# A routed expert layer: f32 matmuls on copied weights against f16 pairs read at the expert's address

## The reference

```python
def _L2_ffn_ref(x, Wr, br, W1, b1, W2, b2):        # (2, 1024) tokens, H=256, F=1024, 8 experts
    probs = softmax(x @ Wr + br); gate = probs * keep      # keep: top-p 0.8
    h = relu(einsum('bth,ehf->betf', x, W1) + b1)          # every expert for every token
    y = einsum('betf,efh->beth', h, W2) + b2
    return einsum('bte,beth->bth', gate, y)

def _L3_ffn_ref(x, gate_w, w1, b1, w2, b2):        # x: layernormed rows
    router_probs = softmax(x_flat @ gate_w)
    expert_idx = argmax(router_probs); expert_w = router_probs[expert_idx]
    for e in range(8):                              # one expert for each token
        h = gelu(x_flat @ w1[e] + b1[e])            # exact gelu
        y = h @ w2[e] + b2[e]
        out = out + where(expert_idx == e, expert_w, 0)[:, None] * y
...
x = x + _L2_ffn_ref(_layernorm(x), ...)
x = x + _L3_xattn_ref(_layernorm(x), ctx_1024, ctx_1024, ..., fside, ...)
x = x + _L3_ffn_ref(_layernorm(x), L3_ffn_gate_w, L3_ffn_w1, L3_ffn_b1, L3_ffn_w2, L3_ffn_b2)
```

## Time and profile before

| | us |
|---|---|
| median of 3 runs | 3391.13 |
| the profiled execution's own time | 3388.76 |
| its span | 3387.2 |
| TensorE busy | 2920.6 (86%) |
| VectorE busy | 2081.2 (61%) |
| ScalarE busy | 1898.3 (56%) |
| POOL busy | 1309.0 (39%) |

### The profile page before, as it was taken

The page is one execution under the profiler, slowest core; times in us unless marked ns, Lnnn a source line. Parts: engine busy times, 40 slices in busy tenths (PEclk is TensorE's granted clock), DMA queues, the critical chain, the costliest instruction groups (busy, mean ns, idle before and its releaser), DMA issues. The chain is left out here.

```text
span 3387.2 us, 67815 instructions
## 1 busy us (share of the span) xinstructions
PE 2920.6 (86%) x26424; PEld 2022.7 (60%) x26425; DVE 2081.2 (61%) x3113; ACT 1898.3 (56%) x2879; POOL 1309.0 (39%) x944
## 2 busy tenths in 40 slices
PE   6769998746979998979998597979999999998596
PEld 3246665424536666446667596766666666667595
DVE  6968887577968883968873223855444444466222
ACT  3448886283658884658884012855555555466131
POOL 2249998020248884148883213810000000055212
PEclk8979998877979999989998798979999999998698
DMA  4611111200022220022222412011000000052512
GB/s 140 230 57 55 54 56 59 91 13 13 1 56 54 57 48 15 1 60 54 54 48 105 153 37 52 2 51 30 26 26 26 26 26 1 1 117 68 213 36 70
DMA packets 218051, 193.17 MB, mean 57 GB/s; under 512 B 126837, under 2 KB 176866, under 8 KB 216738
## 3 DMA queue, kind: packets, MB, share of 16 engines
q1 hardware_dynamic: 210247, 172.30, 17.6%
q0 software_dynamic: 5280, 14.42, 1.3%
q10 hardware_dynamic: 2233, 2.39, 0.2%
HBM read 112.72 MB, written 39.00 MB: 45 GB/s over the span
## 5 line engine op out<-in xcount | busy, mean ns | idle before, releaser
L2667 POOL TENSOR_TENSOR lta_p_lo<-lta_p,lta_p_hi 128x1024 f16<-128x1024 f32 x256 | 538.7, 2131 | 214.7 <-DVE lta_p_hi L2790 214.7
L2862 ACT ACTIVATE lta_p<-lta_banks,lw_gmax 128x512 f32<-128x512 f32 x512 | 323.7, 682 | 110.2 <-PE lta_banks L2705 106.8
L2773 DVE TENSOR_REDUCE lta_s_ps<-lta_s_ps 128x1 f32<-128x1101 f32 x240 | 314.0, 1308 | 102.2 <-PE lta_s_ps L2683 102.2
L3964 PE MATMUL m_y_ps<-m_w,m_hT 128*128 128x256 f16 x3072 | 357.4, 273 | 2.3 <-DVE m_hT L4122 2.3
L3952 PE MATMUL m_h_ps<-m_x,m_w 128*128 128x512 f16 x1536 | 353.2, 380 | 3.7 <-issue 3.7
L4122 DVE TENSOR_TENSOR m_hT<-m_h,m_hT 128x512 f16<-128x512 f32 x256 | 176.8, 692 | 278.8 <-ACT m_hT L4049 277.1
L4049 ACT ACTIVATE m_h<-m_h_ps,m_h_bias,m_h_scale 128x512 f32<-128x512 f32 x256 | 199.3, 778 | 263.7 <-PE m_h_ps L3952 255.5
L3964 PEld LDWEIGHTS m_y_ps<-m_w,m_hT 128*128 128x128 f16 x3072 | 299.9, 98 | 66.1 <-issue 8.1
L1242 POOL TENSOR_TENSOR c0a_tri_p_lo<-c0a_tri_p,c0a_tri_p_hi 128x1024 f16<-128x1024 f32 (+2 forms) x192 | 285.6, 1525 | 58.5 <-DVE c0a_tri_p_hi L1416 57.6
L3952 PEld LDWEIGHTS m_h_ps<-m_x,m_w 128*128 128x128 f16 x1536 | 150.4, 98 | 160.2 <-issue 6.2
L1491 ACT ACTIVATE c0a_tri_p<-c0a_banks,c_size 128x512 f32<-128x512 f32 (+3 forms) x384 | 208.2, 576 | 45.6 <-PE c0a_banks L1310 33.1
(11 more groups left out here) (768 smaller groups left out, 6522.0 us busy)
## 6 DMA issues: line engine op xcount, KB each, us to landing
m_w<-in_L_ffn_w_dram SPq DMA_DIRECT2D x4, 8192.0 KB, 39.0
m_raw<-in_L_ffn_W_dram SPq DMA_DIRECT2D x16, 1024.0 KB, 6.6
lta_q<-ltb_qT SPq DMA_DIRECT2D x96, 128.0 KB, 2.4
c_side<-in_fside_Bx16xSxS_dram SPq DMA_DIRECT2D x16, 616.0 KB, 4.7
c0a_tri_q<-c_near SPq DMA_DIRECT2D x96, 96.0 KB
c0a_tri_k<-c_mixed SPq DMA_DIRECT2D x93, 96.0 KB
lta_k<-ltb_kT SPq DMA_DIRECT2D x64, 137.6 KB, 2.5
lt_vh<-ltb_v SPq DMA_DIRECT2D x64, 128.0 KB
```

The lines of the kernel that those rows point to most:

```text
L2667: nc.gpsimd.tensor_tensor(p_lo[:, slot, :], p32[:, p32_slot(h, j), :], p_hi[:, slot, :], ALU.subtract).then_inc(rested, 1)
L2773: nc.vector.tensor_reduce(ntop_of(h)[:, n:n + 1], scores(h, n), AX_X, ALU.max, negate=True).then_inc(top_ready, 1)
L2862: nc.scalar.activation(p32[0:rows, slot, c * 512:(c + 1) * 512], t_ps[0:rows, c, :], ACT.Exp, bias=bias, scale=p["gmax"][0:rows, 0:1]).the ...
L3964: last = nc.tensor.matmul(y_ps[:, q, 0:D], hT[:, k % 2, a, f, q * P:(q + 1) * P], w2[:, v, b, f, :], start=f == 0 and m == 0, stop=f == FC ...
```

## The change

The last layer is built anew as `paired_routed_stage`; `combine_experts` is removed.

1. A class `PairWeights` splits the last layer's w1 and w2 in f16 halves during m2, one expert each four steps: POOL loads both raw matrices and stores the halves in DRAM (1 MB each), VectorE does two reductions of 128x2048 and one small, eight small size operations and two splits of 128x2048, ScalarE two halvings of 128x2048. m2's own first split moves from the third step of an expert to the end of the second.
2. During c3, SP loads all w1 halves (8.4 MB) and b2 (1 MB) behind the third side load; in c3o it stores x to a row table in DRAM.
3. `route_rows` does layernorm and routing in one block. It stores the normalised rows and the token's weight to the same table (a row is 256 + 256 + 1 numbers), computes for each of the 23 x 128 places the token that stands there (from one-hot tables by sixteen small matmuls), and POOL gathers the first seven tiles; SP loads w2 halves of the first three.
4. `paired_experts` is a list of 23 tiles without a loop instruction. w1 is read at the expert's address as the stationary operand, w2 from a ring of three; all products are three f16 matmuls. VectorE multiplies with the token's weight and adds x, and POOL scatters the rows straight to the output.
5. One of the two `sorted_x` buffers and its zero fill at the program's start go.

```diff
+    def load_expansion(self, sp):
+        sp.dma_start(self.w1[:], self.dram[0].rearrange("e p n -> p e n")).then_inc(self.w1_loaded, 16)
+        sp.dma_start(self.b2[:], self.w("b2").partition_broadcast(P)).then_inc(self.b2_loaded, 16)
+    def load(self, pool, e):
+        if e:
+            pool.wait_ge(self.split_done, 2 * e)
...
+    def halve(self, act, e, k):
...
+        self.nc.scalar.activation(self.pair[k][:, 0, :], self.raw[k][:], ACT.Identity, scale=self.down[:, k:k + 1]).then_inc(self.halved, 1)
+    def split(self, dve, e, k):
+        dve.wait_ge(self.halved, 2 * e + (k + 1))
+        self.nc.vector.scalar_tensor_tensor(self.pair[k][:, 1, :], self.raw[k][:], self.down[:, k:k + 1], self.pair[k][:, 0, :],
+                                            ALU.mult, ALU.subtract).then_inc(self.split_done, 1)
```

In `route_rows`, the end of POOL's list (XS_RING is 7, W2_RING 3):

```diff
+        pool.wait_ge(pairs.x_stored, 16 * (TILES // 4))
+        pool.wait_ge(rows_stored, 16 * (TILES // 4))
+        pool.wait_ge(w_stored, 16)
+        pool.wait_ge(ids_ready, 1)
+        for j in range(XS_RING):
+            gather_rows(nc, pool, r, j)
```

In `paired_experts`:

```diff
+        def expand(j):
+            e = pe.value_load(r["expert_of"][0:1, j:j + 1], min_val=0, max_val=E - 1)
...
+            for f in range(FC):
+                for c in range(DC):
+                    for m, (a, b) in enumerate(PAIRS_OF_HALVES):
+                        last = nc.tensor.matmul(h_ps[:, u, f * P:(f + 1) * P], w1[:, bass.ds(e, 1), a, c, f * P:(f + 1) * P].rearrange("p a n -> p (a n)"), x16[:, u, b, c, :],
...
+        def reduce(j):
+            pe.wait_ge(r["w2_loaded"][k], 16 * (j // W2_RING + 1))
...
+                for m, (a, b) in enumerate(PAIRS_OF_HALVES):
+                    last = nc.tensor.matmul(y_ps[:, u, 0:D], hT[:, u, a, f, :], w2[:, k, b, f, :],
...
+        for j in range(NT):
+            if j + 2 < NT:
+                turn(j + 2)
+            if j + 1 < NT:
+                expand(j + 1)
+            reduce(j)
...
+            nc.gpsimd.indirect_dma_start(out, bass.IndirectOffsetOnAxis(ap=r["ids"][:, j:j + 1], axis=0),
+                                         ys[:, j % 2, :], None).then_inc(ys_stored[j % 2], 16)
+            if j + XS_RING < NT:
+                gather_rows(nc, pool, r, j + XS_RING)
```

In m2, VectorE's list (k is the step, `more` says that m2 has a next expert):

```diff
-                    if more and k % CHUNKS == 2 and q < 2:
-                        split_weights(e, ev, q)
+                    if k % CHUNKS == 1 and q == 1:
...
+                        routed.largest(dve, 2 * i + k // CHUNKS, 0)
+                    if k % CHUNKS == 1 and q == 2:
+                        routed.largest(dve, 2 * i + k // CHUNKS, 1)
+                        routed.largest(dve, 2 * i + k // CHUNKS, 2)
+                    if k % CHUNKS == 1 and q == 3:
+                        if more:
+                            split_weights(e, ev, 0)
+                        routed.sizes(dve, 2 * i + k // CHUNKS)
+                    if more and k % CHUNKS == 2 and q == 0:
+                        split_weights(e, ev, 1)
+                    if k % CHUNKS == 2 and q > 1:
+                        routed.split(dve, 2 * i + k // CHUNKS, q - 2)
```

More of the change, by code:

```diff
@@ L215, in _, with add_projection_stage @@
                         gate(t)
-def add_projection_stage(nc, env, tag, rows, weight, bias, beside=None):
+def add_projection_stage(nc, env, tag, rows, weight, bias, beside=None, routed=None):
     with ExitStack() as ctx:
@@ L3288, in _ @@
[L3288 to L3300 removed]
+        r = {}
@@ L3403, in _ @@
                 bias.load(sp, g)
+        if routed is not None:
+            routed.load_expansion(sp)
     @block.gpsimd
```

474 lines of the change are left out of this document (435 added, 39 removed).

## The result

| kernel | median us | range | runs |
|---|---|---|---|
| before | 3391.02 | 3390.62 to 3391.66 | 4 |
| changed | 3346.26 | 3343.56 to 3349.20 | 4 |

The ratio is 0.9868 (95% interval 0.9851 to 0.9885): the change saves 45 us, not the 74 of the forecast, and the time lies above the forecast's range. The profiled execution took 3345.36 us; its span is 3343.7.

What follows compares the result with a forecast made beforehand. TensorE was taken to be busy throughout the gated layer and the expert loop. Terms of -8.3, -1.2, -38.0, -27.7 and +1.0 sum to -74.2: 3388.76 becomes 3314.6, plus 2.37 gives 3317 us; range 3306 to 3343.

Steps and rivals of the forecast that it cites:

- Up to the logits nothing changes: Ahead of the expert loop: the time to the logits stays as before, with logits ending about 3143.8.
- Start of the loop, -8.3: From the logits to the first expansion, which was to start at 3175.6 instead of 3183.89; bounds -11 and -2.
- The block ends without waiting for them: End of the routing block: it does not wait for the seven gathers, so the next block starts at 3172.2.
- First expansion, -1.2: Loop's first expansion: 48 f16 matmuls at half clock take 5.4 us instead of 6.6.
- Loop, -38.0: From the first expansion's end to the last matmul's: 125.8 us instead of 163.8; bounds -39.3 and -7.
- The sequencer needs no more than 31 + 30 = 61 ns for a matmul: Loop's expansion: TensorE's sequencer time per matmul, register operations included, where the array needs 56 ns.
- TensorE doesn't keep 56 ns: Rival for the loop: register operations slow the expansion, 3349 if none is hidden, 3333 for half; chance 0.13.
- Tail, -27.7: From the last matmul to the end of the span: 5.2 us instead of 32.9; bounds -29 and -25.9.
- Gated layer +0.5, attention +0.5: Added weight splitting and loads in these two layers cost 0.5 us each; bounds 0 to +86 and 0 to +5.
- The rival with 86 us on the path: Gated layer: VectorE's 86 us of new work come to stand on TensorE's path, giving 3403; chance 0.03.
- ScalarE sets the pitch: Rival for the loop: ScalarE's work per tile passes the 5.6 us pitch; 0.5 us over gives 3328; chance 0.10.
- Transfers set the pitch: Rival for the loop: 1.4 MB of transfers make a tile take 6.6 us, giving 3339; chance 0.10.

Runs made afterwards that it cites:

- gate_first: Changed kernel with the router's weights loaded in the attention, ahead of the f16 matrices, instead of at the routing block's start; 3337.35 us, ratio 0.985.
- the aligned rows: Three runs of the changed kernel with table rows of 2560, 2112 and 2080 bytes instead of 2052; 3344.31, 3337.23 and 3336.46 us.
- gathers_later: Changed kernel with all seven gathers issued at the start of the tiles' block, not at the end of the routing block; 3337.93 us, ratio 0.9856.
- fixed_expert: Changed kernel with w1 read at a constant address per tile, without the expansion's register operations, output not the tile's own expert; 3331.74 us, ratio 0.9828.
- all_four: Changed kernel with router weights loaded early, gathers in the tiles' block, expansion and reduction matmuls alternating, and 2560-byte rows filled in the gated layer; 3318.88 us, ratio 0.9796.
- rows_aligned: Changed kernel with table rows of 2560 bytes instead of 2052, the unused rest filled once during the attention; 3344.31 us, ratio 0.9873.
- tail_plain: Changed kernel with the last tile's rows stored plainly by SP to a spare table, left out of the output; 3340.78 us, ratio 0.9854.
- helpers_twice: Changed kernel with four more 128x2048 VectorE reductions per expert in the gated layer, about 73 us in all; 3350.68 us, ratio 0.9883.

## Why the prediction was wrong

The direction and the sources of the gain were right. Three terms of the sum were too good and one was missing, and the range was built as if at most one would fail: the likeliest case's own range (3307 to 3328) took in none where several do, and 3346.26 lies 3.3 above the whole one. Its lower end doesn't follow either: the good bounds of start and tail, 2.7 and 1.3 below what was taken, lead to 3313.

- *"Up to the logits nothing changes"*: this step failed outright, by 9.1 us, and no rival held it. The prediction counted the weight column's small pieces as a risk, but not what the same queue carries before the router's weights. The rows' stores were called "outside the path"; their pieces of 1 KB at a stride of 2052 bytes made them last until after the layernorm. `gate_first` takes the wait away by the order (24.2 instead of 32.7), the aligned rows by the stores' own time (24.3, 24.2, 24.2).
- *Start of the loop, -8.3* (measured -5.1, inside its bounds of -11 and -2). The step that failed is "The block ends without waiting for them", the gathers. The 2.3 us were rightly read as running from the landing of the last scatter, but were put behind the last gather's issue. The next block started 6.9 us after that issue's end and 1.3 after the landing. Before, it was 6.9 after the last issue's end too; that this agrees is chance, since in `gate_first` it is 4.1 after the issue, and again 1.3 after the landing. Part of the miss was made up for: the ids came 15.9 us after the logits, where the working gives 17.2. The sign "if POOL's gathers start later than 3163" was met, at 3172.4, mostly by the wait ahead of the logits. `gathers_later` shows the end of the block as the cause.
- *First expansion, -1.2*: measured -1.4.
- *Loop, -38.0* (measured -26.2, bounds -39.3 and -7). "The sequencer needs no more than 31 + 30 = 61 ns for a matmul" failed. The 30 was right (0.8 us for 24). But the 46 ns of the earlier trace rows are the operation's record, not its pitch: with the matmuls behind it, it takes 124 ns, so 48 matmuls take the sequencer 4.1 us or 86 ns each. "It can catch up during the reduction" was right in kind: it gains 1.1 us, and needs 4.1 - 2.69 = 1.4 and the time for the expert's number, which the prediction left out. The 21 expansions behind the second one took 3.23 us on average instead of 2.75, which is 10.1 of the 11.8 us, and the second, without the lead, 1.1 more than 2.75. The 0.45 taken for half clock were 0.2, in one turn; the last wait of 0.63 and small parts make the rest. The rival "TensorE doesn't keep 56 ns" is thus what came about, and the mark "wrong if matmuls of the expansion come at over 60 ns" was met, at 66.7. The rule of the Trainium skill ("TensorE: Matmul & The Clock Gate", "Back-to-back issue gap"), about 81 ns for such a stream, isn't what acts here: without register operations it is 56 over groups of 48 (`fixed_expert`).
- *Tail, -27.7* (measured -22.6, beyond its bound of -25.9 by 3.3): "then an indirect store" was taken for the end. What was left out stands behind the landing: 0.2 us to the drain, the drain's 3.2, and 1.7 from there to the end of the span. Ahead of the scatter 0.6 more went by than was taken, with 0.8 of waiting for the scatter before; its landing took 3.1 of the 3.8 taken.
- *Gated layer +0.5, attention +0.5*: measured -0.8 and +0.3. The rival with 86 us on the path is refuted; with 73 us more of such work the layer itself still took 719.6, and 3.6 came behind it.
- *ScalarE sets the pitch*: refuted, since ScalarE keeps up even with 5.52 us a tile. Its groups in the loop, the counterpart of the earlier trace rows:

```profile
L3718 ACT ACTIVATE m3e_h<-m3e_h_ps,pw_b,m_h_in 128x128 f32<-128x128 f32 x184 | 69.0, 455 | 30.1 <-PE m3e_h_ps L3671 30.1
L3722 ACT ACTIVATE m3e_hT<-m3e_h,m_h_down 128x512 f16<-128x512 f32 x46 | 33.2, 722 | 1.5
```

  Eight gelus take 3.0 us, two halvings 1.44. A gelu with a scale from memory beside its bias reads 455 ns instead of 382, and adds (69.0 - 50.0) / 184 = 103 ns of busy time. The Trainium skill, "ScalarE: Activation LUTs", section "What ACT_TABLE_LOAD costs", has 93 ns for such an operand; the trace's 103 of busy time is near it, and the mean durations differ by 73.
- *Transfers set the pitch*: refuted. The second matrices land in 5.0 us with three buffers, no reduction in the middle of the loop waits for them, and 257 GB/s were moved without loss.

## What to carry to other kernels

A small load that TensorE waits for belongs ahead of the bulk on its queue, and a table in DRAM that is written in 1 KB pieces should have rows of a whole number of 32 bytes, the least that was found good here. Matmuls whose weights are read at a register's address cost the sequencer 124 ns for each register operation; sum up the sequencer's round of a loop as one does an engine's, and alternate such short matmuls with long ones. Where a block ends behind an indirect transfer, its end waits for the landing: put the transfer at the start of the next block where the wait is longer than the block's switch. Two kernels can agree in the time from an issue and still wait for the landing; a third, in which the landing is shorter, tells the two apart.

## What was not expected of the hardware

- Stores of 0.5 MB in pieces of 1 KB to DRAM landed in 10.2 and 20.5 us at a stride of 2052 bytes, and in 2.9 to 3.4 at 2080, 2112 and 2560 bytes. In the loop, gathers from the same rows at 2052 bytes went on in a stretch of 233 GB/s without being waited for.
- POOL's drain at the routing block's end ended 0.34 us after the landing of the last gather in eight profiles, 3.2 to 6.2 us after the end of its issue. At the program's end it starts 0.2 us after the last scatter's landing and ends 5.6 us after its issue's end in ten profiles, 6.15 in `gathers_later` and `all_four`. It can't be seen in the semaphores' waits; it stands only among the sequencer's instructions.
- A register operation that reads 46 ns holds TensorE's sequencer for 124 with the one or two matmuls behind it. It costs nothing where two matmul records of 216 ns stand behind each, as in the loop before, and 0.55 us for 32 of them between matmuls of 56.
- The length of the first 2244 to 2251 us of the program varies between profiles by more than `rows_aligned`, `tail_plain` or `helpers_twice` change the total. Small effects were therefore read from the interval that the edit touches.
